# TensorE's other work in a state-space scan, laid behind each half feed, and a turned sum copied by ScalarE alone

## The reference

```python
u, z = jnp.split(xn @ W_in, 2, axis=-1)
u2 = silu(conv(u) + conv_b)
dbl = u2 @ W_x                            # dt_low (16), Bm (16), Cm (16)
dt = softplus(dbl[..., :16] @ W_dt + b_dt)
A = -exp(A_log)                           # 512 channels x 16 states
def step(h, inp):                         # over the 512 tokens
    dA = exp(dt_t[:, :, None] * A)
    h = dA * h + (dt_t * u_t)[:, :, None] * B_t[:, None, :]
    return h, einsum('bdn,bn->bd', h, C_t)
y = (ys + u2 * D) * silu(z)
x + y @ W_out
```

## Time and profile before

| what | value |
|---|---|
| median of 3 runs | 1571.45 us (1570.2 to 1573.3) |
| the profiled execution's own time | 1569.42 us |
| its span | 1567.6 us |
| PE busy | 1435.7 us (92%) |
| DVE busy | 1068.8 us (68%) |
| ACT busy | 854.0 us (54%) |
| POOL busy | 477.9 us (30%) |
| granted clock of PE, mean | 0.962 of full speed |

### The profile page before, as it was taken

How to read it: one execution, slowest core, us unless ns; L and a number is a source line. 1 busy time by engine, 2 the same in 40 slices (tenths; PEclk the granted TensorE clock), 3 DMA queues, 4 the chain that set the end, 5 groups by cost and what they waited for, 6 DMA issues and landing times.

```text
span 1567.6 us, 20191 instructions
## 1 busy us (share of the span) xinstructions
PE 1435.7 (92%) x7399; PEld 980.7 (63%) x7404; DVE 1068.8 (68%) x1218; ACT 854.0 (54%) x1509; POOL 477.9 (30%) x140
## 2 busy tenths in 40 slices
PE   5898799689998989979998889999989999999997
PEld 3576333389797979643444333333368888888886
DVE  6997395899989899774343567777463565555655
ACT  2433456699999998532333278787632533333332
POOL 0999120089898888200332220000000000000000
PEclk7899999799999999999999999999999999999999
DMA  7110010511413211411213032443000000000000
GB/s 271 26 62 1 1 54 2 197 47 55 158 58 122 81 55 54 152 21 20 61 41 91 21 101 58 130 136 95 1 1 0 1 14 1 0 14 1 14 1 14
DMA packets 36624, 87.61 MB, mean 56 GB/s; under 512 B 8350, under 2 KB 24948, under 8 KB 32948
## 3 DMA queue, kind: packets, MB, share of 16 engines
q1 hardware_dynamic: 36532, 86.39, 16.5%
HBM read 68.10 MB, written 18.21 MB: 55 GB/s over the span
## 4 chain that ended last, share of the span: by engine, by line
PE 71%; DVE 10%; ACT 9%; DVEq 5%; issue 3%; POOL 1%; DMA 0%; ACTq 0%; SPq 0%
PE ps L1452 12%; PE ps L1461 12%; PE ps L1018 5%; PE ps L1320 4%; PE ps L1393 4%; PE ps L1187 4%; PE ps L1003 3%; ACT arena L1756 3%; DVE arena L2057 3%; ACT arena L1744 3%; PE ps L1308 3%; DVEq L2056 2%; PE ps L1004 2%; PE ps L1213 2%; PE ps L896 2%
## 5 line engine op out<-in xcount | busy, mean ns | idle before, releaser
L2619 POOL TENSOR_TENSOR arena<-arena 128x2048 f32<-128x2048 f32 x63 | 287.9, 4585 | 140.8 <-DVE arena L2157 139.7
L2157 DVE TENSOR_TENSOR_SCAN arena<-arena,ps 128x1024 f32<-128x1024 f32 x128 | 284.6, 2272 | 28.3 <-issue 19.4
L1756 ACT ACTIVATE arena<-arena,mam 128x511 f32<-128x511 f32 x256 | 166.1, 714 | 22.5 <-DVE arena L2157 22.5
L1934 ACT ACTIVATE arena<-ps,rho 128x512 f32<-128x512 f32 x256 | 158.9, 688 | 34.0 <-PE ps L1393 32.6
L2391 DVE TENSOR_REDUCE mxs<-ps 128x1 f32<-128x512 f32 x224 | 141.1, 684 | 45.0 <-PE ps L1308 43.1
L1003 PE MATMUL ps<-early,arena 128*128 128x128 f32 x768 | 129.6, 277 | 15.4 <-DVE arena L2157 10.3
L1963 ACT ACTIVATE arena<-arena 128x256 f32<-128x256 f32 x192 | 85.5, 500 | 81.6 <-DVE arena L2562 50.3
L1452 PE MATMUL ps<-early,arena 128*128 128x256 f32 x512 | 127.1, 380 | 2.9 <-DVE mam L2558 1.8
L2599 POOL TENSOR_TENSOR arena<-arena 128x4096 f32<-128x4096 f32 x16 | 115.0, 7189 | 43.3 <-DVE arena L2076 43.3
L1744 ACT ACTIVATE arena<-arena,early 128x512 f32<-128x512 f32 x192 | 124.1, 712 | 3.9 <-DVE arena L2135 3.9
L1461 PE MATMUL ps<-arena 128*128 128x256 f32 x512 | 121.0, 379 | 1.2 <-issue 1.2
(11 more groups left out here) (349 smaller groups left out, 2471.1 us busy)
## 6 DMA issues: line engine op xcount, KB each, us to landing
arena<-bc_scratch SPq DMA_DIRECT2D x32, 512.0 KB, 3.7
arena<-in_ffn SPq DMA_DIRECT2D x8, 1024.0 KB, 4.9
batch_scratch<-arena SPq DMA_DIRECT2D x2, 3072.0 KB, 9.4
arena<-batch_scratch SPq DMA_DIRECT2D x6, 1024.0 KB, 6.8
arena<-q_scratch SPq DMA_DIRECT2D x96, 64.0 KB, 2.2
arena<-k_scratch SPq DMA_DIRECT2D x96, 64.0 KB, 2.2
arena<-in_dec_w SPq DMA_DIRECT2D x1, 3855.0 KB, 16.1
arena<-in_cond SPq DMA_DIRECT2D x1, 3739.5 KB, 11.5
```

The source lines that it names most:

```text
L1756: last = act.activation(decay[:, (2 * k + h) % 3, i, 1:S], dt[b % 2][:, m, 1:S], ACT.Exp, scale=a_neg[:, m * NS + n:m * NS + n + 1])
L1934: act.activation(pt[:, j % 4, i], ps[:, 3 + (hg + n) % 3, :], ACT.Exp, scale=rho[:, 0:1]).then_inc(s_pt, 1)
L2157: dve.tensor_tensor_scan(half, view(decay[:, (2 * k + h) % 3], [[1, 2 * S]]), view(ps[:, FEED + 2 * h, :], [[1, 2 * S]]), 0.0, ALU.mult, A ...
L2619: pool.tensor_tensor(state[:, k % SLOTS], state[:, k % SLOTS], view(c_rows[:, j % 2, k % G, :], [[0, M], [1, S]]), ALU.mult).then_inc(s_hc, 1)
```

## The change

PE's loop is cut in halves: half of the other work comes behind each half feed, in place of all of it behind both. `mamba_half` does two of the four chunks of `mamba_out`, the first of them waiting for banks 0 and 1 alone, the second for 2 and 3. `sum_half` sums two tiles of a state (units 2k and 2k+1), so that the sum may be at half a state. At n = 5 two states are summed in place of one, and at most two halves behind each half feed after that. `turn_back` stays behind the second half feed. ACT copies all four banks, in two operations, between the two decays of n = 3, where it copied two banks ahead of the decays of n = 4; DVE no longer copies (except after the loop, where nothing changes). DVE adds the first residual ahead of `scan(k, 0)` of n = 4, where it was between the two scans.

```diff
--- before.py
+++ after.py
@@ -955,14 +955,13 @@
                                         ident[0:64, 0:64])
                 last.then_inc(s_bt_mm, 1)
 
-            def d_term(b, n):
-                if b >= 2 and n == D_FROM:
+            def d_term(b, n, h):
+                if b >= 2 and n == D_FROM and h == 0:
                     pe.wait_ge(s_back_u2, 16 * (b - 1))
-                for m in range(M // 2 * (n % 2), M // 2 * (n % 2 + 1)):
-                    t = (n - D_FROM) // 2
-                    last = pe.matmul(ps[:, t, m * P:(m + 1) * P], u2[b % 2][:, m, t * P:(t + 1) * P], diag[:, m, :],
-                                     start=False, stop=False, skip_group_check=True)
-                if n == NS - 1:
+                t, m = (n - D_FROM) // 2, 2 * (n % 2) + h
+                last = pe.matmul(ps[:, t, m * P:(m + 1) * P], u2[b % 2][:, m, t * P:(t + 1) * P], diag[:, m, :],
+                                 start=False, stop=False, skip_group_check=True)
+                if n == NS - 1 and h == 1:
                     last.then_inc(s_dterm, 1)
 
             pe.wait_ge(s_mam, 32)
@@ -1005,12 +1004,16 @@
                                      dub[:, k % 2, TILES - 1, 0:P], start=True, stop=True)
                 last.then_inc(s_dbu, 1)
 
-            def sum_state(k):
-                if k < B * NS - 1:
-                    pe.wait_ge(s_hc, k + 1)
+            def sum_half(unit):
+                k = unit // 2
+                if unit % 2 == 0:
+                    if k < B * NS - 1:
+                        pe.wait_ge(s_hc, k + 1)
+                    else:
+                        pe.wait_ge(s_ends, 2)
+                    sum_tiles(k, (2, 3))
                 else:
-                    pe.wait_ge(s_ends, 2)
-                sum_tiles(k, range(TILES)).then_inc(s_y, 1)
+                    sum_tiles(k, (0, 1)).then_inc(s_y, 1)
 
             def sum_tiles(k, tiles):
                 for t in tiles:
@@ -1027,40 +1030,45 @@
                         last = pe.transpose(ps[:, m, t * P:(t + 1) * P], zT[b][:, t, m * P:(m + 1) * P], ident)
                 last.then_inc(s_g_turned, 1)
 
-            def mamba_out(b, o, bank):
+            def mamba_half(b, o, bank, half):
                 if o == 0:
-                    pe.wait_ge(s_g01, b + 1)
-                    pe.wait_ge(s_g23, b + 1)
+                    pe.wait_ge(s_g23 if half else s_g01, b + 1)
                 g = view(zT[b], [[S, M], [1, S]])
-                for m in range(M):
+                for m in (2 * half, 2 * half + 1):
                     last = pe.matmul(ps[:, bank, :], w_out[:, m, o * P:(o + 1) * P], g[:, m, :],
                                      start=(m == 0), stop=(m == M - 1))
-                last.then_inc(s_out_mm, 1)
+                if half:
+                    last.then_inc(s_out_mm, 1)
+
+            def mamba_out(b, o, bank):
+                mamba_half(b, o, bank, 0)
+                mamba_half(b, o, bank, 1)
 
             due = 0
             for k in range(B * NS):
                 b, n = divmod(k, NS)
-                feed(k, 0)
-                feed(k, 1)
-                if b and n == 2:
-                    turn_back(b - 1)
-                elif b and n == 3:
-                    mamba_out(b - 1, 0, 0)
-                elif b and n == 4:
-                    mamba_out(b - 1, 1, 1)
-                elif b and n == 5:
-                    pe.wait_ge(s_hc, due + 1)
-                    sum_tiles(due, (2, 3))
-                    pe.wait_ge(s_x1, C * b + 1)
-                    sum_tiles(due, (0, 1)).then_inc(s_y, 1)
-                    due += 1
-                else:
-                    for _ in range(2):
-                        if due <= k - 2:
-                            sum_state(due)
-                            due += 1
+                for h in range(2):
+                    feed(k, h)
+                    ready = 2 * (k - 2 + h)
+                    if b and n == 2:
+                        if h:
+                            turn_back(b - 1)
+                    elif b and n in (3, 4):
+                        mamba_half(b - 1, n - 3, n - 3, h)
+                    elif b and n == 5:
+                        if h:
+                            pe.wait_ge(s_x1, C * b + 1)
+                        sum_half(due + h)
+                        sum_half(due + h + 2)
+                        due += 4 * h
+                    else:
+                        at_end = n == 1 or k >= B * NS - 2
+                        for _ in range(4 if at_end else 2 if ready - due > 2 else 1):
+                            if due < ready:
+                                sum_half(due)
+                                due += 1
                     if n >= D_FROM:
-                        d_term(b, n)
+                        d_term(b, n, h)
             C2, F8 = (5, 6), (7, 4)
 
             def modulated(b):
@@ -1088,8 +1096,9 @@
                     last = pe.matmul(ps[:, 4, o * B:(o + 1) * B], w2c[:, c, o * P:(o + 1) * P],
                                      style2[:, 2, c, :], start=(c == 0), stop=(c == C - 1))
             last.then_inc(s_prep_mm, 1)
-            sum_state(due)
-            sum_state(due + 1)
+            assert due == 2 * (B * NS - 2)
+            for unit in range(due, 2 * B * NS):
+                sum_half(unit)
             pe.wait_ge(s_scan, 2 * B * NS)
             modulated(0)
             turn_back(B - 1)
@@ -1760,6 +1769,8 @@
             def turned_back(b):
                 act.wait_ge(s_g_turned, b + 1)
                 act.activation(view(zT[b], [[S, 2], [1, S]]), ps[:, 0:2, :], ACT.Copy).then_inc(s_g01, 1)
+                if b < B - 1:
+                    act.activation(view(zT[b], [[S, 2], [1, S]], 2 * S), ps[:, 2:4, :], ACT.Copy).then_inc(s_g23, 1)
 
             for i in range(B):
                 softplus_parts(i, 0)
@@ -1784,9 +1795,9 @@
             for k in range(B * NS):
                 if k:
                     times_b(k)
-                if k > NS and k % NS == 4:
+                decays(k, 0)
+                if k > NS and k % NS == 3:
                     turned_back(k // NS - 1)
-                decays(k, 0)
                 decays(k, 1)
 
             def styled(b):
@@ -2182,16 +2193,12 @@
 
             for k in range(B * NS):
                 b, n = divmod(k, NS)
-                if b and n == 5:
-                    residual(b - 1, 1)
+                if b and n in (4, 5):
+                    residual(b - 1, n - 4)
                 scan(k, 0)
-                if b and n == 4:
-                    residual(b - 1, 0)
                 scan(k, 1)
                 if b and n == 1:
                     gate_y(b - 1)
-                if b and n == 2:
-                    turned_back(b - 1)
                 if b == B - 1 and n >= 6:
                     linear_weights(n - 6)
 
```

## The result

| what | before | after |
|---|---|---|
| median of the runs shown together | 1571.34 us (1570.2 to 1573.3, 4 runs) | 1555.35 us (1548.83 to 1558.29, 4 runs) |
| ratio to before, 95% interval | | 0.9891 (0.9859 to 0.9922) |
| the profiled execution's own time | 1569.42 us | 1552.41 us |
| its span | 1567.6 us | 1550.6 us |
| gate to gate, first and second full sequence | 82.71, 82.74 us | 77.46, 77.44 us |

The account below looks back on a forecast made before the run. ACT was taken to bound the first sequence and PE's work and waits each boundary; 2 x 5.3 + 3.4 = 14.0 us off 1571.45 gave 1557.5 us, range 1555 to 1561, or 1554.5 to 1563.5 with the first rival and its mix.

Parts of the forecast that it names:

- Steps 1 to 3: Boundary's start: turn_back unmoved, copies' delays covered, halves of mamba_out start the fourth state's feed 2.3 us earlier.
- Step 4: Boundary up to n = 9: PE stays the bound, and the feed of n = 9 starts 4.1 us earlier.
- Step 5: From n = 9 to the gate: DVE runs at 4.40 us a state, making a full sequence 5.3 us shorter.
- The entry that was called least certain: ACT's lead from n = 9: 2.3 us against 1.6 eaten; entered as nothing, bounds nothing and 1.6 us a sequence.
- Step 6: Last sequence: the scan of n = 9 starts 38.4 us after the gate, not 41.85, a gain of 3.4 us.
- Step 7: First sequence, the end, POOL and SP: nothing to gain, no extra instructions; entered as nothing.
- the scatter outside the scan: The run's scatter, entered as 1.5 us in the forecast's own range.
- ACT as the bound behind the boundary: Rival, chance 0.13: ACT binds behind the boundary, costing 1.6 us in each of two full sequences; 1560.8 us.
- The waits in front of `mamba_out`: Rival, chance 0.04: ACT's copies come late in the boundary, losing step 3's 2.3 us three times; 1564.3 us.
- the halves buy nothing: Rival, chance 0.03: PE's work, not its order, bounds the boundary, and POOL's products give gains back; 1571 us.
- a refill without a wait: Rival, chance 0.02: every half feed on PE pays a refill of 0.22 us, together 3.5 slower, 1575.
- The clock: Rival, chance 0.01: PE's clock falls to 1.2 GHz in the boundary; with 6 us a boundary, 1575.5 us.

Follow-up runs that it names:

- experiment 4: PE's halves from the changed kernel; ACT, DVE's copy and DVE's first residual from the kernel before; 1563.96 us median, ratio 0.9954, profiled execution 1569.65.
- the second measurement: The changed kernel run once more with no edit; 1553.25 us median, ratio 0.9896 to the kernel before.
- the memsets: The changed kernel with one, then three DVE memsets more in front of the first scan; 1554.98 us, ratio 0.9908, and 1551.19 us, ratio 0.9898.
- full456: The changed kernel, in n = 4, 5 and 6 ACT multiplies dt*u's fourth tile in full and PE only transposes it; 1548.65 us, ratio 0.9868.
- 3: The kernel before with only ACT's copies of all banks amid the decays of n = 3, PE's order whole; 1566.84 us, ratio 0.9985.
- 5 to 9: From the changed kernel: 5 halves in boundary only, 0.9937; 6 halves everywhere else, 0.9952; 7 is full456; 8 ACT operations added, 0.9939; 9 copies later, 0.9926.
- experiment 9: The changed kernel with ACT's two copies behind both decays of n = 3, 1.2 us later; 1558.91 us, ratio 0.9926.

## Why the prediction was right or wrong

**Steps 1 to 3, the copies and the half pieces: right.** `turn_back` ended in time, ACT's copies started 4.4 and 5.3 us after the gate (4.4 and 5.4 were asked for), L1038 at 5.7 (5.8), and the fourth state's feed at 10.3 (407.3 - 397.04 = 10.3). The cover of ACT's second decays and of its next products held: only one scan waits for ACT in the whole boundary, 0.58 us. That the place of the copies decides was seen twice: 1.2 us later costs 1.1 a sequence, and with the copies on DVE and ACT as before the profiled scan gained nothing from the halves (it would have gained 3.8 had the clock held, by the 1.6 a boundary of experiment 4).

**Step 4, the catching up: right.** The feed of n = 9 starts 36.56 after the gate; the layout said 433.6 - 397.04 = 36.6. DVE's idle in front of single scans is 0.57 where 0.65 was reckoned.

**Step 5, n = 9 to the gate: right, and for the reason given.** Twenty scans in 44.02 us. With the order whole again in these states it went back to 4.6 a state. The entry that was called least certain held with less to spare than it might look: a lead of 2.3 less 1.6 should leave 0.7; it was 0.5.

**Step 6, the last sequence: right within 0.1.** The scan of n = 9 starts 38.5 after the gate, where 38.4 was laid out; 3.31 us came, where 3.4 was entered.

**Step 7 and the sum: the step that failed.** In the scan 13.86 of 14.0 us came, so the mechanism held. The time came out 16.0 lower by the medians and 17.1 by the ratio: 1571.45 x 0.9891 = 1554.3, under both low ends that the prediction gave, 1555 and 1554.5, and in the second measurement the median, 1553.25, lies 1.2 under the lower of them. The term that was mis-sized is the scatter outside the scan, entered as 1.5 us on the strength of three runs of the kernel before; it was the only term that could take the time below the forecast, to 1556.0, for the others, ACT's 1.6 and the refills, point upward. Measured, the kernel before goes from 1562.5 to 1573.3 in 63 executions, and the changed kernel's eight go from 1548.8 to 1558.3: the two slowest have a mean granted clock of 0.959, the three fastest 0.965 to 0.967. Step 7 entered nothing for the work outside the scan, and there the first two profiles differ by 3.1 us: 2.2 ahead of DVE's last product before the scan, where no edited instruction has run, 1.2 behind the product of the last state, and 0.2 the other way between.

Whether a part of this belongs to the change stays open. The intervals of the two ratios are 12.3 to 22.2 and 13.8 to 18.8 us and both hold 13.9, so the surplus is not clear of noise. The four profiles of the changed kernel's program, those with the memsets counted, have 1322 to 1324 us outside the three spacings, and the two of the kernel before 1327 and 1329; the seven of the other kernels have 1325 to 1329. What lies outside has edited instructions only in the first sequence and in the sums and `mamba_out` behind the last state, and the clock rows show where some of it goes: from 200 to 280 us behind the last product the granted clock differs, in work that no edit touches. An effect of some 2 us by shifting this work against the clock would fit, but full456 has as much of PE's new order and 1325, and the ratios of the experiments exceed what their spacings give by -1.2 to +3.2 us, the memsets set aside, with intervals as wide; the halves alone exceed it by 8.2, since their profiled execution was their slowest.

**The rivals.** ACT as the bound behind the boundary did not come, by half a microsecond; full456 has reached it. The waits in front of `mamba_out` went. That the halves buy nothing is answered by 3: from the copies alone to the whole change the scan gains 10.4 of the 13.9 us. That step has DVE's first residual in its new place too, which no run tests by itself. No feed paid a refill without a wait: at 405.35 it follows L1038 without a gap. (The price of this rival was summed a little low: 3 x 0.6 and 2 make 3.8, not 3.5.) The clock kept 1.00 in all boundaries of the changed kernel, though `mamba_out` is cut up among transposes, and so had the stretch of the first sequence before, where 28 of the 36 to 40 records of a state are transposes. The rule of the Trainium skill ("TensorE: Matmul & The Clock Gate", Part 4: PE-mode transpose), that the full clock does not engage for transposes as they do not count as PE-busy in the same way, is not what the traces show here. The clock fell only behind the longest waits, those of 3.02 us in experiment 4.

## What to carry to other kernels

When one engine serves a chain of short steps and long side work, put the side work in pieces no longer than the chain's own step, behind each step, and bring the data that the first piece waits for early: a piece that waits in front of a step holds the chain itself. With the copies moved the halves brought 10.4 of the 13.9 us; with the copies where they were, the profiled scan was 1.0 us longer. Draw the sequence anew from one trace's start-to-start times; it gave each spacing of the change within 0.1 us, and those of experiments 3 and 5 to 9 within 0.4. Take the range of the whole, though, from how much executions of a kernel differ, and from many of them: outside the scan the thirteen profiles here differ by 7 us.

## What the runs showed of the hardware that was not expected

In each boundary of the halves alone (experiment 4) PE waited 3.02 us and worked again, and then the granted clock was 0.50, which is 1.2 GHz, for some 3.4 us, beginning when PE had been back at work for 0.3 to 1.4 us. It cost 1.6 us: 2.51 us for four records of 512 columns where 1.88 is usual, 0.85 for three transposes where 0.49 is. A wait of 0.89 us in the same place (experiment 9), and those of 0.86 behind the gate in the changed kernel, were followed by the upper clock throughout. A wait can so cost more than its length, here half as much again.

The stretch behind the scan took 923.1 to 928.6 us in four profiles of the changed kernel's program, and was shortest in the one that had 3.7 us more to do in front of it. It is one profile each: the four executions with that work go from 1549.2 to 1560.3. Over 80 us of this stretch the mean granted clock was 0.94 to 0.96 in five of the thirteen profiles and 0.87 in the other eight, in the same work.
